# A decoder layer on one core: a staging tile for each half of a weight matrix, the output weights split inside the first batch, and z tiles transposed in a new order

## The reference, cut to what matters

```python
x = x + attention(layernorm(x), Wq, bq, Wk, bk, Wv, bv, Wo, bo, slopes)     # 16 heads of 32, ALiBi, softmax
x = x + xattn(ctx, ctx, layernorm(x), ssm_kernel, D)                        # 32 heads of 8
x = x + moe(layernorm(x), router_gate, expert_gate_up, expert_down)         # 8 experts, top 2
...
kv = jnp.einsum('bhil,bhjl->bijhl', k_, v_)
kv_f = jnp.fft.rfft(kv, n=fft_size)
kernel_f = jnp.fft.rfft(ssm_kernel, n=fft_size)
y = jnp.fft.irfft(kv_f * kernel_f, n=fft_size)[..., :L]
out = y + kv * D[None, None, None, :, None]
out = jnp.einsum('bijhl,bhil->bjhl', out, q_)
```

## Time and profile before

| | |
|---|---|
| median of 3 runs | 1629.73 us (1624.77 to 1634.55) |
| the profiled execution's own time | 1625.41 us |
| its span, first to last instruction | 1623.7 us |
| PE busy | 1473.8 us, 91% of the span |
| DVE, ACT, POOL busy | 1041.0, 765.4, 648.8 us |
| mean granted TensorE clock | 0.938 of full speed |

### The profile page before, as it was taken

One profiled execution on the slowest core, in us unless ns is written; L12 is line 12 of the kernel. 1 busy time (PEld: TensorE's weight loads), 2 busy tenths in 40 slices (PEclk: granted clock), 3 DMA queues, 4 the chain that ended last, 5 costly groups with the idle time before them and its releaser, 6 DMA issues. The chain is left out here.

```text
span 1623.7 us, 32907 instructions
## 1 busy us (share of the span) xinstructions
PE 1473.8 (91%) x8665; PEld 1190.9 (73%) x8666; DVE 1041.0 (64%) x3154; ACT 765.4 (47%) x2010; POOL 648.8 (40%) x834
## 2 busy tenths in 40 slices
PE   5899999999999999968999799996963999999997
PEld 4788888888888788746777677776962777777775
DVE  4777777777777777756888788887664233332232
ACT  3777777776767677743322223221332323333322
POOL 3011111111111111015888368872764555555553
PEclk9999999999999999988999999996556999999999
DMA  5543433344334443456211341113883555555652
GB/s 160 127 115 100 102 85 100 91 104 103 99 91 104 104 104 91 120 208 229 53 52 52 129 148 53 52 33 133 180 206 70 104 102 99 98 99 98 102 101 44
DMA packets 89729, 172.24 MB, mean 106 GB/s; under 512 B 26336, under 2 KB 26336, under 8 KB 88608
## 3 DMA queue, kind: packets, MB, share of 16 engines
q1 hardware_dynamic: 59840, 115.12, 26.8%
q0 software_dynamic: 18176, 35.80, 12.4%
q10 hardware_dynamic: 11616, 20.27, 4.1%
HBM read 78.10 MB, written 44.79 MB: 76 GB/s over the span
## 5 line engine op out<-in xcount | busy, mean ns | idle before, releaser
L1149 PE MATMUL ps_y<-pairs,taps 128*128 128x288 f32 x1280 | 311.6, 406 | 7.0 <-DVE prods L1275 3.8
L1149 PEld LDWEIGHTS ps_y<-pairs,taps 128*128 128x128 f32 x1280 | 242.7, 190 | 75.4 <-issue 8.7
L860 ACT ACTIVATE probs<-neg_scores,neg_max 128x256 f32<-128x256 f32 x512 | 255.2, 505 | 26.6 <-DVE neg_max L661 26.6
L661 DVE CUSTOM_DVE_ANT_0 neg_scores<-ps_scores,alibi 128x256 f32<-128x256 f32 x512 | 194.9, 418 | 90.2 <-PE ps_scores L526 61.6
L870 ACT ACTIVATE probs_t<-ps_probs_t 128x512 f32<-128x512 f32 x208 | 124.1, 597 | 130.2 <-PE ps_probs_t L537 130.2
L1623 POOL DMA_INDIRECT out<-y_row,back x72 | 113.3, 1573 | 170.2 <-DMA out<-y_row,back 134.2
L537 PE MATMUL ps_probs_t<-ident,probs 128*128 128x128 f32 x1024 | 159.3, 280 | 9.1 <-ACT probs L860 9.1
L410 POOL COPY inv_wide<-inv_sum 128x512 f32<-128x512 f32 x32 | 20.6, 675 | 316.9 <-DVE inv_sum L677 316.9
L2026 DVE TENSOR_TENSOR st_lo<-ps_x,st_hi 128x512 fp32r<-128x512 f32 x72 | 49.8, 692 | 145.9 <-ACT st_hi L1798 145.8
L1180 ACT ACTIVATE q_ring<-q_g 128x512 f32 (+1 forms) x64 | 40.2, 630 | 215.8 <-DVE ps_y L1268 204.8
L537 PEld LDWEIGHTS ps_probs_t<-ident,probs 128*128 128x128 f32 x1024 | 124.3, 143 | 22.9 <-ACT probs L860 9.5
(11 more groups left out here) (197 smaller groups left out, 3596.7 us busy)
## 6 DMA issues: line engine op xcount, KB each, us to landing
q_stack<-q_hi SPq DMA_DIRECT2D x128, 128.0 KB, 2.3
k_stack<-k_hi SPq DMA_DIRECT2D x128, 128.0 KB, 2.3
taps<-kernel_pad SPq DMA_DIRECT2D x64, 256.0 KB, 3.1
x_in<-in_x SPq DMA_DIRECT2D x16, 512.0 KB, 3.3
q_stack<-q_lo SPq DMA_DIRECT2D x64, 128.0 KB, 2.3
k_stack<-k_lo SPq DMA_DIRECT2D x64, 128.0 KB, 2.3
x_rows<-x_mid SPq DMA_DIRECT2D x16, 512.0 KB, 2.9
ctx_g<-in_ctx_t SPq DMA_DIRECT2D x2, 4096.0 KB, 12.2
```

Source lines behind the costliest of these rows:

```text
L661: last = dve.tensor_tensor_reduce(neg_scores[h % 2][:, tt, :], ps_scores[h % 2][:, tt, :], alibi[h % 2][:, P - P * tt:P - P * tt + T], -Q_ ...
L860: last = act.activation(probs[h % 2][:, tt, :], neg_scores[h % 2][:, tt, :], ACT.Exp, bias=neg_max[par][:, h, tt:tt + 1], scale=-1.0, accu ...
L1149: last = pe.matmul(ps_y[par][:, lc, :].rearrange("p (b q) -> p b q", b=GB)[:, :, 0:PAIRS], taps[r][:, block_cols:block_cols + P], pairs[r] ...
```

## The change

It has two parts that do not touch each other.

**The weights' staging.** Every half gets a tile of its own or one that is long free again: halves 0 to 5 go to `w_in[0]`, `w_in[1]`, `inv_wide`, `x_mid[1]`, `w_in[0]`, `w_in[1]`, halves 6 and 7 (Wo) to `o_norm` and `inv_b`, which the first batch does not use yet. Only Wv's halves wait for a tile. x of batch 1 is loaded behind Wv instead of ahead of Wq. DVE's set-up is put in another order, and Wo is split inside the first batch: ACT's part ahead of heads 3 and 5, DVE's part in heads 4 and 6. New waits: POOL's bias add of the first two batches waits for `w_ready` 4, the first output projection and the first write of `inv_b` for `w_ready` 8.

**The z tiles.** They are transposed in the order `Z_ORDER`, the eight even tiles first. For these PE waits for the folds of heads 0 to 15 alone, and for the DVE's last reading of the bank that a tile goes to (`halved`). The odd tiles wait for all folds, as all did before. DVE adds the tiles in the same order.

```diff
+            halves = [(w, half) for w in (wq, wk, wv, wo) for half in range(2)]
+            staged = [w_in[0][:], w_in[1][:], inv_wide[:], x_mid[1][:], w_in[0][:], w_in[1][:],
+                      one_tile(o_norm), one_tile(inv_b)]
+            WO_HI_SLOTS, WO_LO_SLOTS = (3, 5), (4, 6)
...
                 load_x(0, 0)
-                load_x(0, 1)
...
+                for n, src in enumerate((wq_t, wq_t, wk_t, wk_t, wv_t, wv_t, wo_t, wo_t)):
+                    half = n % 2
+                    if src is wv_t:
+
+                        sp.wait_ge(w_ready, half + 1)
...
+                    if n == 5:
+                        load_x(0, 1)
...
+                        if not has_before and h in WO_LO_SLOTS:
+                            split_lo(6 + WO_LO_SLOTS.index(h))
...
+                        if not has_before and h in WO_HI_SLOTS:
+                            split_hi(6 + WO_HI_SLOTS.index(h))
...
+            Z_ORDER = list(range(0, GT, 2)) + list(range(1, GT, 2))
...
-                    pe.wait_ge(z_ready, (g + 1) * SH + Z_START)
-                    for t in range(GT):
-                        bank = ps_y[t % 8 // EC][:, t % EC, :]
-                        pe.wait_ge(x2_ready, g * GT + t + 1 - 8 + X2_START)
+                    pe.wait_ge(z_ready, g * SH + SH // 2 + Z_START)
+                    for j, t in enumerate(Z_ORDER):
+                        bank = ps_y[j % 8 // EC][:, j % EC, :]
+                        if j == 0 or j == EC:
+
+                            pe.wait_ge(halved, (g + 1) * SH - 1 + j // EC + HALVED_START)
+                        if j == GT // 2:
+
+                            pe.wait_ge(z_ready, (g + 1) * SH + Z_START)
+                        if j >= 8:
+
+                            pe.wait_ge(x2_ready, g * GT + j + 1 - 8 + X2_START)
```

More of the change, by code:

```diff
@@ L193, in build_decoder @@
             stack_load = [sem(f"stack_load{r}") for r in range(HPC)]
-            w_load = [sem(f"w_in_load{i}") for i in range(WEIGHT_BUFS)]
+            w_load = [sem(f"w_in_load{i}") for i in range(8)]
             w_hi_ready = sem("w_hi_ready")
@@ L301, in _ @@
                 load_x(0, 0)
-                load_x(0, 1)
[L303 to L319, removed]
+                for n, src in enumerate((wq_t, wq_t, wk_t, wk_t, wv_t, wv_t, wo_t, wo_t)):
+                    half = n % 2
+                    if src is wv_t:
+                        sp.wait_ge(w_ready, half + 1)
+                    if src is wo_t:
+                        by_quad = src.rearrange("(c r d) f -> c d r f", c=EC, r=HPC)
+                        for c in range(EC):
+                            sp.dma_start(staged[n][c * DH:c * DH + DH, :, :],
+                                         by_quad[c][:, 2 * half:2 * half + 2, :]).then_inc(w_load[n], 16)
+                    else:
+                        sp.dma_start(staged[n], src.rearrange("(h c p) f -> h p c f", h=2, p=P)[half]).then_inc(w_load[n], 16)
+                    if n == 5:
+                        load_x(0, 1)
                 sp.wait_ge(free_row_step, 2)
@@ L390, in add_output_bias @@
                     wait_apart(pool, x_load[par], k * 16 + 16, passed)
-                    if not (isinstance(k, int) and k == 0):
+                    if isinstance(k, int) and k == 0:
+                        pool.wait_ge(w_ready, 4)
+                    else:
                         wait_apart(pool, x1_stored[par], k * 16, passed)
@@ L508, in output_rows @@
                     if piece == 0:
+                        if is_first(k, par):
+                            pe.wait_ge(w_ready, 8)
                         pe.wait_ge(o_lo_kept, batch(k, par) * HPC + HPC)
@@ L712, in x1_statistics, with split_lo @@
                     dve.tensor_copy(all_moments[:, ds(b * TT, TT), :], x1_moments_of[:]).then_inc(x1_moments, 1)
+                def split_lo(n):
+                    w, half = halves[n]
+                    dve.wait_ge(w_hi_ready, n + 1)
+                    dve.tensor_tensor(w[1][:, 2 * half:2 * half + 2, :], staged[n],
+                                      w[0][:, 2 * half:2 * half + 2, :], ALU.subtract).then_inc(w_ready, 1)
                 def step(k, par, has_before, has_after, has_after_next):
@@ L754, in _ @@
                     normalise(0, 0, tt)
[L755 to L765, removed]
                 split_lo(0)
@@ L788, in _ @@
                 split_lo(5)
+                for tt in range(TT):
+                    token_stats(0, 1, tt)
                 for half in range(2):
                     keep_k_lo(0, 0, half)
-                split_lo(6)
-                split_lo(7)
+                for tt in range(TT):
+                    normalise(0, 1, tt)
                 dve.wait_ge(alibi_step, 4)
@@ L875, in keep_inverses @@
                         act.wait_ge(inv_spread, batch(k, par) * 2 + (half + 1))
+                        if is_first(k, par):
+                            act.wait_ge(w_ready, 8)
                         act.activation(inv_b[:, 2 * half:2 * half + 2, :], ps_proj[:, half, :], ACT.Copy)\
@@ L884, in keep_o_hi, with split_hi @@
                             .then_inc(o_hi_kept, 1)
+                def split_hi(n):
+                    w, half = halves[n]
+                    act.wait_ge(w_load[n], EC * 16 if w is wo else 16)
+                    act.activation(w[0][:, 2 * half:2 * half + 2, :], staged[n], ACT.Copy).then_inc(w_hi_ready, 1)
                 def step(k, par, has_before, has_after, has_after_next):
@@ L920, in _ @@
                 act.dma_start(kernel_row[:, P:], ssm_kernel).then_inc(small_load, 16)
[L921 to L928, removed]
                 split_hi(0)
@@ L943, in _ @@
                     keep_v(0, 0, tt)
-                split_hi(6)
-                split_hi(7)
                 exponentials(0, 0, 0)
-                act.wait_ge(w_ready, 8)
+                act.wait_ge(w_ready, 6)
                 act.wait_ge(free_rows_store, 16)
@@ L1022, in build_decoder @@
             QUADS = SH // PAIR_BUFS
+            Z_ORDER = list(range(0, GT, 2)) + list(range(1, GT, 2))
+            assert T == 2 * P and GT == 16
             def by_head(tile):
```

15 lines of the change are left out of this document (7 added, 8 removed).

## The result

The changed kernel takes 1613.98 us (median of 5 runs, 1613.42 to 1616.26) against 1629.73 before; the ratio is 0.9906, 95% interval 0.9886 to 0.9925. Forecast was 1615.5, range 1609 to 1624. Its profiled execution took 1613.98 us, with a span of 1612.2.

The account below looks back on a forecast made before the run. PE was taken to pace the batches, with waits at the start and both group ends to remove. Gains of 5.5, 4.25 and 4.2 us sum to 13.95; 1629.7 less 14 gives about 1615.5, range 1609 to 1624.

Parts of the forecast that it names:

- Steps (1) to (3): Set-up: first Q product near 17.0, K at 25.6 instead of 29.0, `k_lo` done at 34.2 against 36.9.
- step (2): Set-up on PE: Q's 48 products need some 8.6 us and end at 25.6, where K starts instead of 29.0.
- later clock rise in Q: Q's products in the set-up: one deduction in the start's lower bound, 0.5 us.
- lower bound: Start: a gain of only 1 us, with longer POOL chain (1.8 less), Wo half uncovered (2.3), slower Q (0.5).
- Step (4): SP's transfers before the scores: first k transfer issued at 34.2, third 1.2 us later; scores possible at 38.7.
- step (5): PE's K and V: 11.45 us from 25.6 plus a 1.4 us pause of V, ending at 38.5.
- Step (6): DVE before the first maximum: POOL's chain 5.3 us, normalising 2.91, ALiBi 0.74; maximum at 40.85 against 46.36.
- Step (7): Wo splits in heads 3 to 6: costed at nothing; uncovered, up to 4.5 us together.
- Step (8): PE's clock around the first scores: should stay at full speed with 0.3 to 1 us idle; no gain counted.
- rival D: First batch: PE's clock stays at 0.50 throughout, making the kernel slower, near 1638 us; chance 0.03.
- The group ends: End of each group: 16 adds without a gap behind the halving, gaining 4.25 us in group 0, 4.2 in group 1.
- Rival B: Group ends: PE slow, 0.85 us a tile for twelve tiles; gain 3.0 us each, 1618.2 in all; chance 0.12.

Follow-up runs that it names:

- x_early: The changed kernel with batch 1's statistics moved ahead of `q_lo` and x of batch 1 loaded behind Wk: 1607.68 us, ratio 0.9878 to the kernel before.

## Why the prediction was right, step by step

**Steps (1) to (3), the set-up.** The first Q product came at 16.90 (17.0 foretold), the pause of V was 1.09 (1.4), `k_lo` was done at 32.9 (34.2 foretold, though the step's own terms, 31.6 and 1.00, 0.84, 1.00, add up to 34.4). The mis-sized term is step (2): Q was taken at 8.6 us from the trace of before and took 7.19 (16.90 to 24.09). A product takes 0.41 us at first and 0.28 after; the slow ones went on for 5.9 us in the trace of before (18.52 to 24.41), for 2.9 here (16.90 to 19.81), for 4.8 in the changed kernel's run beside x_early (16.84 to 21.67). There K began at 24.80 and the first maximum came at 40.01, in the first trace at 24.09 and 39.29: both 15.2 us behind K. The prediction has 15.25 (25.6 to 40.85). So 1.5 of the 1.6 us between forecast and first trace come from Q. Why the first products are slow, and for how long, stays open: the granted clock is 1.00 in the slow stretch (17.0 to 19.6) as in the fast one (20.0 to 24.0), so the "later clock rise in Q" of the lower bound is shown by no run. Part of the 1.5 is luck. Q's 8.60 us in the trace of before are the longest of all traces, the 7.19 in the first trace of the changed kernel the shortest; over five traces with this set-up the first maximum lies between 39.29 and 40.20, over three with the old one between 46.36 and 46.77.

What the prediction does not say is that the change puts Q on the path. Before, K began at 28.9 to 29.0 in all three traces, with Q at 7.5, 7.7 or 8.6 us, since it waited for `q_lo` behind batch 1's normalising. Now K follows Q at once, and the first maximum comes 15.2 us behind K in all five traces, so that every tenth of Q counts.

**What was late last before** was read from one trace: the third k transfer, used at 45.40. The kernel before also holds the first scores until all eight halves are split (`pe.wait_ge(w_ready, 8)` ahead of `scores(0, 0, 0)`), a wait that the change drops and the prediction does not mention. In the first trace it was met at 44.43, when `wo_lo` was done (42.07 plus 2.36). In the second trace of the kernel before, and in that of the z tiles alone, it ended last:

```profile
45.99 0.89 PE L526 MATMUL ps_scores<-k_stack,q_stack 96*128 96x256 f32 x4 [4.03 <-DVE wo_lo L761]
```

So Wo held up the start in two ways, in SP's queue and through its splits, and the change ends both. With Wo's split in the set-up again, but without that wait, the first maximum came at 41.25, still 5.1 us ahead of 46.36. How the gain divides among Wo, the other tiles and DVE's order was not tried further.

**Step (4)** held: SP's transfers did not limit the first maximum; the k transfers were issued from 33.0 on, and PE wrote the first scores at 36.85 (38.5 foretold by step (5), with Q too long), 2.4 us ahead of the first maximum.

**Step (6)** held within 0.3 us: chain 5.5 us (5.3 foretold), normalising 2.90 (2.91), ALiBi 0.73, maximum right behind it. That the normalising's 2.9 us come from POOL's bias add is shown by the add held back and by x_early. What it costs depends on what DVE does next: held back, the add fell on ALiBi.

**Step (7)**, the Wo splits at no cost, is consistent with the first batch of staging alone, 38.63 us, and of the first look at `x_early`, 38.27, both with the splits inside, against 38.62 before without them. It was not tested apart from the clock, which stood near 0.50 for a part of that batch in most traces. With Wo in the set-up instead the first maximum was 2 us later.

**Step (8)** was wrong: PE's idle ahead of the maxima was 2.5 us, not 0.3 to 1 (the prediction's own steps (5) and (6) put the maximum 2 us behind the scores), and the clock fell to 0.66 in 40 to 45, in another trace to 0.50 in 45 to 50. That first batch took 42.12 us instead of 39.09, so PE does count there. It is a small form of rival D, 3 us, and not shown to be a doing of the change: the kernel before had 38.62 and 41.32.

**The group ends** gave 4.43 and 4.37 us (4.25 and 4.2 foretold): 16 adds without a gap, the odd tiles' folds done in time. Rival B is answered, though not by the reason given against it. Its condition occurred: in group 0 the 16 early transposes did not keep PE fast, which restarted behind the halving as slowly as it had behind the last fold before. Windows of the kernel before, then of the changed kernel (us, busy us by engine, then granted clock, DMA share, GB/s):

```profile
911.50:914.00 2.50, 2.50 (x12) 2.50 (x13) 1.29 (x2) 0.52 (x1) 2.50 (x3) 0.50 0.00 0
...
900.50:903.00 2.50, 2.50 (x12) 2.50 (x13) 2.50 (x5) 0.00 (x0) 2.21 (x3) 0.52 0.02 6
```

Both show 12 transposes, three tiles, in 2.5 us. In group 1 the granted clock was 1.00 at that place, and the adds took the same 9.6 us. What made the slowness free is that DVE had four finished tiles, 2.4 us of adding, in hand, and that only some three tiles were slow, not the twelve of B's price. With only four tiles ahead PE's restart, again at 0.50, came when DVE had nothing left, and the gaps were back: 1.21, 0.16 and 0.17 us.

**The sum** in the traces is 7.07 plus 8.8, 15.9 us, in the medians 15.75; foretold were 13.95. In the traces the difference is nearly all Q's length. The medians cannot tell: the ratio's interval, 0.9886 to 0.9925, is a gain of 12 to 19 us, and that 15.75 agrees so well with the traces' sum is luck.

## What to carry to other kernels

When a gap on an engine is to be filled, look first at when its data lands: counted from Q's end, the same move brought the first maximum forward by 2.0 us with x behind SP's wait, and by 3.0 with x issued ahead of it. A wait that keeps two engines apart pays only if nothing behind it meets the same partner; finishing the partner's work earlier took away both collisions at once. Where a set-up runs at PE's start, take its length, and which wait ends last there, from several traces, since those of one are not those of the next. When a long wait goes, ask what had been hidden behind it: here Q's length. And work kept in hand for the engine that sets the pace can cover a slow restart of another.

## What was not expected of the hardware

**Clock.** The first batch took 39.1, 42.0 and 42.1 us in three traces of the changed kernel and 38.3, 38.3 and 41.2 in three of `x_early`. The long ones are those in which the granted clock was at 0.50 to 0.52, its 1.2 GHz level, through 45 to 50. With the same pauses ahead of it the clock fell in one execution and stayed at 1.00 in two.

**Loop ends.** From the third batch on two batches make one turn of a loop, and a turn's end costs something that no batch inside it has. The kernel before, windows inside a turn and at its end:

```profile
168.00:211.00 43.00, 42.05 (x343) 35.52 (x341) 34.13 (x119) 30.18 (x93) 7.78 (x20) 1.00 0.40 99
211.00:216.00 5.00, 2.36 (x19) 1.88 (x16) 2.40 (x7) 4.11 (x13) 2.77 (x3) 0.96 0.17 52
216.00:221.00 5.00, 5.00 (x33) 5.00 (x33) 4.95 (x16) 5.00 (x17) 0.00 (x0) 0.70 0.15 56
```

PE stands still for 2.6 of 5 us at the turn's end, and its clock is 0.70 in the next 5 us. The first 1/sums of two batches lie 41.3 to 41.5 us apart inside a turn and 43.1 to 45.8 across its end, over all traces. In the trace above PE waits there for DVE's `xn_t_lo` (1.94 and 0.70 us); what would shorten it was not tried.
